# Chunk attention's values products on 128 keys by 128 queries, with block-diagonal probabilities, in a four-layer transformer kernel

## The chip, the cores and the metric

The kernel runs on one core of one Trainium2 chip. The metric is the device time of one launch in microseconds (us). The time before is 2157.64 us, the median of three runs (2156.42 to 2162.59).

## What is computed

The input is 16 sequences of 256 tokens with 128 features. Four attention blocks follow each other, each with a residual and a feed-forward block behind it: banded ("band"), causal, chunked ("chunk") and low-rank ("lowrank"). The chunk block has 16 heads of 8 features, and a token sees only the 64 tokens of its own chunk:

```python
B, T, C = x.shape            # 16, 256, 128
H, cs = (N_HEAD, CHUNK)      # 16, 64
d = C // H
nc = T // cs
...
scores = jnp.einsum('bnqhd,bnkhd->bnhqk', q, k) * scale
p = jax.nn.softmax(scores, axis=-1)
y = jnp.einsum('bnhqk,bnkhd->bnqhd', p, v)
y = y.reshape(B, T, C)
return jnp.einsum('btc,oc->bto', y, w_proj)
```

Two layers follow as `x + attention(layernorm(x))` and `x + ffn(layernorm(x))`; the second feed-forward block (behind chunk and lowrank) quantises its input and its hidden values to 4 bits in blocks of 16.

## The kernel before

A **unit** is one attention block of one sequence: 16 units each of band (B0 to B15 below), causal (C0 to C15), chunk (K0 to K15) and lowrank (L0 to L15), and 16 of "end" (E0 to E15), which hold only the last feed-forward. A unit first runs the feed-forward that precedes its attention ("forward" and "finish": `xT`, `ffn` 1 and 2, `hid`, for the quantised one `quant` and `ffn` 3, then `down`, `res`), then its queries, keys and values ("operands": `xn`, `xT`, `qk`, `rope`, `cast`, `stack`, `v`), the maxima of the scores ("maxima": `score` fills and DVE's reductions, then `parts`), the attention ("back": `nm`, the scores again as `S`, exponentials, the values products `V`), and the "tail" (`ctx`, `ctxT`, `out`). Units of different kinds run interleaved: while K5 is in its back, the forward of L3 runs.

**The order** of the steps on each engine is written out before the kernel is built. `make_plan` walks six queues (the stages) per engine with a table of assumed costs (`work`), the dependences (`needs`) and a table of leads (`LEAD`, one number for each engine, stage and kind of unit, and `PER_UNIT`), and picks each engine's next step. The engines then execute in that order; the assumed costs and the leads decide nothing else. Each PE step that fills PSUM takes one of three slots (`slots`, 1024 columns each), which the reader of the step frees. The values products write to `ctx_ps`, which the ACT step `V` copies to `ctxT`.

**Chunk attention's back**: for each of two 128-token tiles g, `scores` computes all 16 heads: for each head two 64x64 blocks (two chunks), keys on partitions, queries on columns, and on top the negated maxima (`nmT`, `pick`). One ACT instruction takes the exponentials of the whole 128x1024 slot to `probs[:, g % 2, 0]`. `values` then makes, for each head and each chunk, one product of 64 keys (rows) by 32 value columns by 64 queries: 32 products for a tile, 64 for a unit. The value columns hold 8 features and a column of ones, whose product is the denominator.

The trace shows a float32 product as two weight loads and two matmuls, and calls value buffers `band_va`, stacked queries and keys `band_r`. DVE's `nmx<-slots` is the maxima, `x<-slots` on L1317 the last step of an attention unit ("out"), POOL's L644 to L646 the last third of the 4-bit quantisation.

## Time and profile before

| | us |
|---|---|
| median of three runs (lowest to highest) | 2157.64 (2156.42 to 2162.59) |
| the profiled execution: its own time | 2152.07 |
| the profiled execution: span from first to last instruction | 2150.2 |
| PE matmul busy in the span | 1789.7 (83%) |
| PE weight loads busy | 1250.9 (58%) |
| DVE busy | 1345.8 (63%) |
| POOL busy | 978.6 (46%) |
| ACT busy | 808.8 (38%) |
| mean granted TensorE clock | 0.936 |

Shares of the whole span are averages over stages of different make-up; the rows further below are cut by stage. "issue" before a PE row is idle time in which PE waited for nothing that the profile shows. A row's "xcount" may merge instructions of one kind.

### The profile page before, as it was taken

What the parts mean: (1) busy time and instruction counts of PE and PEld (TensorE: products, weight loads), DVE (VectorE), ACT (ScalarE), POOL (GpSimd) and SP (SyncE); (2) the same over time, 40 slices, a digit from 0 to 9 for tenths busy, and PEclk for the clock granted to TensorE, in tenths of its full rate; (3) what the DMA queues carried; (4) which work ended last, traced back from release to release, by engine and by line L of the source; (5) the groups of instructions that cost most, each with busy time, mean ns of one, the idle gap of its engine ahead of it and who ended that gap; (6) DMA issues with size and microseconds to landing.
All of it is one profiled execution on the core that took longest, in us unless ns stands there. A gap on an engine that the chain in (4) does not pass through costs nothing.

```text
span 2150.2 us, 51747 instructions
## 1 busy us (share of the span) xinstructions
PE 1789.7 (83%) x21261; PEld 1250.9 (58%) x21261; DVE 1345.8 (63%) x2753; ACT 808.8 (38%) x1303; POOL 978.6 (46%) x1362
## 2 busy tenths in 40 slices
PE   4899889999999998879999997777776778888883
PEld 4566565666666666655555555667665455555553
DVE  4555555555555543574555555677876788888873
ACT  2333333333333332324444444333333444444441
POOL 3333222333332222453333435689997455555543
PEclk9999999999999999989999999888998788888886
DMA  4000000000000000023333332233443223323310
GB/s 161 1 1 1 1 2 1 1 1 1 1 1 1 1 1 1 16 56 74 64 78 71 75 75 61 60 74 78 91 87 65 46 62 65 65 65 65 65 21 8
DMA packets 167465, 89.54 MB, mean 42 GB/s; under 512 B 9393, under 2 KB 165810, under 8 KB 166978
## 3 DMA queue, kind: packets, MB, share of 16 engines
q1 hardware_dynamic: 167010, 85.70, 18.4%
q8 instruction: 172, 2.82, 0.6%
q14 instruction: 59, 0.48, 0.1%
q0 software_dynamic: 224, 0.54, 0.1%
HBM read 46.36 MB, written 39.85 MB: 40 GB/s over the span
## 4 chain that ended last, share of the span: by engine, by line
PE 51%; DVE 27%; ACT 7%; POOL 7%; issue 6%; DVEq 0%; POOLq 0%; ACTq 0%
PE slots L1327 38%; DVE nmx L1201 12%; PE ctx_ps L1327 10%; DVE rope_part L1242 4%; ACT probs L1087 3%; DVE rope_part L1166 2%; PE slots L1615 2%; ACT ctxT L1007 1%; DVE ctxT L1303 1%; DVE rope_part L1167 1%; POOL xn L922 1%; PE slots L1394 1%; ACT band_va L1023 1%; POOL band_rb L645 1%; DVE band_r L1167 1%
## 5 line engine op out<-in xcount | busy, mean ns | idle before, releaser
L1087 ACT ACTIVATE probs<-slots 128x1024 f32<-128x1024 f32 (+1 forms) x416 | 356.1, 892 | 322.0 <-PE slots L1327 318.8
L1201 DVE TENSOR_REDUCE nmx<-slots 128x8 f32<-128x1024 f32 (+2 forms) x352 | 407.7, 1216 | 102.8 <-PE slots L1327 101.2
L1327 PE MATMUL slots<-band_r 64*64 64x64 bf16 (+4 forms) x5120 | 393.6, 263 | 80.5 <-DVE nmx L1201 41.7
L1327 PEld LDWEIGHTS slots<-band_r 64*128 64x128 bf16 (+2 forms) x5120 | 194.6, 120 | 254.3 <-issue 129.8
L1242 DVE SCALAR_TENSOR_TENSOR rope_part<-slots,bias_qk,rope_band 128x256 f32<-128x256 f32 x512 | 212.3, 477 | 197.3 <-PE slots L1327 176.4
L1327 PE MATMUL ctx_ps<-probs,band_va 64*32 64x64 f32 (+4 forms) x5120 | 260.5, 313 | 42.3 <-issue 19.4
L986 POOL TENSOR_TENSOR band_r<-rope_part 128x512 f32<-128x512 f32 x128 | 164.5, 1285 | 250.9 <-DVE rope_part L1242 250.9
L1327 PE MATMUL slots<-mask,ident_bf 128*128 128x256 bf16 (+1 forms) x896 | 217.2, 324 | 46.9 <-DVE nmx L1201 17.7
L1327 PE MATMUL slots<-nmT,pick 64*128 64x256 bf16 (+2 forms) x2560 | 218.7, 241 | 2.7 <-issue 2.7
L1327 PEld LDWEIGHTS ctx_ps<-probs,band_va 128*32 128x32 f32 (+2 forms) x5120 | 145.3, 118 | 125.6 <-issue 62.8
L900 POOL TENSOR_TENSOR var_eps<-mean_var,eps 128x2 f32<-128x2 f32 x128 | 29.2, 228 | 393.4 <-DVE mean_var L1129 393.4
L1327 PE MATMUL slots<-xT,band_qk 128*128 128x256 f32 x1536 | 200.0, 288 | 8.2 <-DVEq L1248 6.1
L1327 PEld LDWEIGHTS slots<-xT,band_qk 128*128 128x128 f32 x1536 | 188.0, 191 | 19.7 <-DVEq L1248 13.6
L1007 ACT ACTIVATE ctxT<-ctx_ps 128x512 f32<-128x512 f32 (+1 forms) x112 | 87.4, 781 | 169.2 <-PE ctx_ps L1327 169.2
L922 POOL TENSOR_SCALAR band_va<-x,mean_var,rstd 128x128 f32<-128x128 f32 x128 | 100.8, 794 | 86.0 <-PE slots L1368 65.9
L1007 ACT ACTIVATE band_rb<-band_r 128x512 bf16<-128x512 f32 x128 | 79.4, 630 | 157.0 <-POOL band_r L986 157.0
L1327 PEld LDWEIGHTS slots<-mask,ident_bf 128*128 128x128 bf16 x896 | 54.9, 97 | 133.8 <-issue 44.9
L1166 DVE SCALAR_TENSOR_TENSOR rope_part<-band_va,slots 128x352 f32<-128x352 f32 (+2 forms) x128 | 68.6, 536 | 81.9 <-ACT band_va L1023 55.5
L1327 PEld LDWEIGHTS slots<-nmT,pick 64*128 64x128 bf16 (+1 forms) x2560 | 102.9, 104 | 11.5 <-issue 2.9
L922 POOL TENSOR_SCALAR xn<-x,mean_var,rstd 128x128 f32<-128x128 f32 x128 | 103.6, 816 | 2.9 <-POOL rstd L901 2.8
L937 POOL CAST nm<-nmx 128x64 bf16<-128x64 f32 x64 | 15.1, 236 | 179.0 <-PE slots L1573 92.7
L901 POOL TENSOR_TENSOR rstd<-var_eps,minus_half 128x2 f32<-128x2 f32 x128 | 91.5, 715 | 10.0
(181 smaller groups left out, 2947.5 us busy)
## 6 DMA issues: line engine op xcount, KB each, us to landing
band_r<-scratch SPq DMA_DIRECT2D x192, 192.0 KB, 4.5
scratch<-parts SPq DMA_DIRECT2D x96, 192.0 KB, 2.2
scratch<-parts SPq DMA_DIRECT2D x96, 128.0 KB, 2.1
scratch<-parts SPq DMA_DIRECT2D x96, 64.0 KB, 1.8
x<-in_x SPq DMA_DIRECT2D x16, 128.0 KB, 4.5
out<-x SPq DMA_DIRECT2D x16, 128.0 KB, 1.8
band_r<-in_band_qk_a SPq DMA_DIRECT2D x1, 1024.0 KB, 6.4
band_va<-in_band_qk_b SPq DMA_DIRECT2D x1, 1024.0 KB, 10.3
```

Source lines behind the costliest of these rows:

```text
L900: link(nc.gpsimd.tensor_tensor(var_eps[:, b], mean_var[:, b, :, 1], eps[:], ALU.add))
L901: nc.gpsimd.tensor_tensor(rstd[:, b], var_eps[:, b], minus_half[:], ALU.pow).then_inc(rstd_ready, 1)
L922: nc.gpsimd.tensor_scalar(xn[:, t, :], x[:, b, t, :], mean_var[:, b, t, 0:1], rstd[:, b, t:t + 1], ALU.subtract, ALU.mult).then_inc(xn_rea ...
L986: nc.gpsimd.tensor_tensor(band_r[:, b % RING, j], part[:, 0], part[:, 1], ALU.add).then_inc(band_sum, 1)
L1007: return nc.scalar.activation(dst, src, ACT.Copy)
L1087: nc.scalar.activation(probs[:, g % 2, step[2], :, 0:width], slot(u, step).rearrange("p (a n) -> p a n", a=2)[:, :, 0:width], ACT.Exp, sca ...
L1166: link(nc.vector.scalar_tensor_tensor(g_out, t_in, 1.0, gate, ALU.add, ALU.mult))
L1167: nc.vector.tensor_tensor(h_out, g_out, up, ALU.mult).then_inc(free_sem(u, ("ffn", i)), 1)
L1201: nc.vector.tensor_reduce(dst, src, axis=AX.X, op=ALU.max, negate=True).then_inc(free_sem(u, step), 1)
L1242: nc.vector.scalar_tensor_tensor(rope_part[:, c % 2, rot, qk, :], slot(u, step)[:, o:o + TOK], bias_qk[:, j, 2 * qk + rot:2 * qk + rot + 1 ...
L1327: return nc.tensor.matmul(o, lhsT, rhs, start=start, stop=stop, skip_group_check=shared)
L1615: last = nc.tensor.transpose(B[:, g * P:(g + 1) * P], ctxT[:, g, t * P:(t + 1) * P], ident[:])
```

## The change

A chunk unit's exponentials are now two ACT instructions of 64 partitions each, which lay the two chunks' probabilities of a head on the diagonal of a 128x128 block of `probs`; the other half of the block is zero, cleared once for both buffers by a POOL step ("blank") before the first chunk unit and never written again. A values product takes 128 keys by 128 queries for a head: 16 products for a tile where there were 32. ACT's copy of the result loses its permutation. The planner's assumed costs for chunk `S` on ACT and `V` on PE are changed, and every number of `LEAD` and `PER_UNIT`, so that the order of the steps changes from the first units on.

```diff
+FIRST_CHUNK = UNITS.index(("chunk", 0))
...
+        "blank": [("pool", 3.6)],
...
-              ("act", 0.49 if narrow else 0.92)],
-        "V": [("pe", {"band": 2.24, "causal": 0.79, "chunk": 0.61, "lowrank": 1.13}.get(kind))]
+              ("act", 0.49 if narrow else 1.9 if kind == "chunk" else 0.92)],
+        "V": [("pe", {"band": 2.24, "causal": 0.79, "chunk": 0.95, "lowrank": 1.13}.get(kind))]
...
+        if u == FIRST_CHUNK and step == ("S", 0, 0):
+            yield u, ("blank",), "pool"
...
+        if name == "blank":
+            yield FIRST_CHUNK - 1, LAST_V["causal"], "pe"
...
-        "finish": {"causal": -2.336, "chunk": -0.206, "lowrank": -0.262, "end": -0.693},
+        "finish": {"causal": -0.336, "chunk": -0.461, "lowrank": 0.349, "end": -0.388},
...
-PER_UNIT = 0.01
+PER_UNIT = 0.0024
...
+    at = stages["operands"].index((FIRST_CHUNK + 1, ("xn", False)))
+    stages["operands"][at:at] = [(FIRST_CHUNK, ("blank",))]
...
+        def probs_by_head(i):
+
+            return probs[:, i].rearrange("p f a n -> p (f a n)").rearrange("p (h c n) -> p h c n", h=HEADS, c=2)
+
...
+                    if step == ("blank",):
+                        pool.wait_ge(pv_done, gbase[FIRST_CHUNK])
+                        nc.gpsimd.memset(probs[:], 0.0).then_inc(probs_blank, 1)
...
+                        if kind == "chunk":
+                            if u == FIRST_CHUNK and step[1] == 0:
+                                act.wait_ge(probs_blank, 1)
+                            for c in range(2):
+                                rows = slice(c * CHUNK, (c + 1) * CHUNK)
+                                last = nc.scalar.activation(probs_by_head(g % 2)[rows, :, c].rearrange("p (h a) n -> p a h n", a=2),
+                                                            slot(u, step)[rows].rearrange("p (a h n) -> p a h n", a=2, n=CHUNK),
+                                                            ACT.Exp, scale=SD ** -0.5)
+                            last.then_inc(free_sem(u, step), 1)
+                            return
...
-                        elif kind == "chunk":
-                            copy(ctxT[:, 0:4, :].rearrange("p g (t c n) -> p c (g t) n", t=TILES, c=2),
-                                 ctx_ps[:].rearrange("p c (g n) -> p c g n", n=CHUNK)).then_inc(ctx_free, 1)
...
                         for h in range(HEADS):
-                            for cc in range(2):
-                                rows = slice(cc * CHUNK, (cc + 1) * CHUNK)
-                                o = ((h // 4) * TILES + g) * CHUNK
-                                last = mm(ctx_ps[32 * (h % 4):32 * (h % 4) + 32, cc, o:o + CHUNK],
-                                          small_va[rows, b % RING, g, h, :], pr[rows, 0, h % 2, h // 2 * CHUNK:(h // 2 + 1) * CHUNK])
+                            o = ctx_ps[32 * (h % 4):32 * (h % 4) + 32, h // 8, h // 4 % 2 * TOK + g * P:h // 4 % 2 * TOK + (g + 1) * P]
+                            last = mm(o, small_va[:, b % RING, g, h, :], probs_by_head(gi % 2)[:, h].rearrange("p c n -> p (c n)"))
                         last.then_inc(pv_done, 1)
```

What the new order does is seen in rows of the two programs, which give an instruction's line, its output and inputs, and how many follow each other. Line numbers of the changed kernel are higher, for the lines that were added.

**PE, a chunk unit in the middle of the stage, behind K7's `out`.** Before: the feed-forward products `ffn` 1 and 2 of L6 (`fp_gu`), `ffn` 3 of L5 (`ident,band_r`), the two `score` fills of K9 (64x64, x64), `down` of L5 (`fp_d`), then `nm` and the scores of K8:

```order
L1327 MATMUL slots<-fp_gu,xTf 128x352 x12
L1394 MATMUL slots<-ident,band_r 128x128 x2
L1394 MATMUL slots<-ident,band_r 96x128
L1394 MATMUL slots<-ident,band_r 128x128 x2
L1394 MATMUL slots<-ident,band_r 96x128
L1327 MATMUL slots<-band_r 64x64 x64
L1327 MATMUL slots<-fp_d,band_r 128x128 x6
L1573 MATMUL slots<-ident_bf,nm 128x128 x2
L1327 MATMUL slots<-band_r 64x64 x4
L1327 MATMUL slots<-nmT,pick 64x64 x4
```

In the changed kernel, at the same place (again behind K7's `out`):

```order
L1417 MATMUL slots<-ident,band_r 128x128 x2
L1417 MATMUL slots<-ident,band_r 96x128
L1417 MATMUL slots<-ident,band_r 128x128 x2
L1417 MATMUL slots<-ident,band_r 96x128
L1391 MATMUL slots<-ident,band_rb 128x128 x2
L1350 MATMUL slots<-fp_d,band_r 128x128 x6
L1350 MATMUL slots<-fp_gu,xTf 128x352 x12
L1593 MATMUL slots<-ident_bf,nm 128x128 x2
L1350 MATMUL slots<-band_r 64x64 x4
L1350 MATMUL slots<-nmT,pick 64x64 x4
```

`ffn` 3 and `down` of the older feed-forward now stand ahead of `ffn` 1 and 2 of the next one, and nothing stands between `ffn` 2 and `nm`; the two `score` fills are gone from here. The same unit, from the end of its scores to its `out`, before:

```order
L1327 MATMUL slots<-band_r 64x64 x4
L1327 MATMUL slots<-nmT,pick 64x64 x4
L1327 MATMUL slots<-band_r 64x64 x4
L1327 MATMUL slots<-nmT,pick 64x64 x4
L1327 MATMUL ctx_ps<-probs,band_va 32x64 x64
L1327 MATMUL slots<-chunk_qkv,xT 128x128 x6
L1368 MATMUL slots<-ident,xn 128x128 x2
L1615 MATMUL slots<-ident,ctxT 128x128 x8
L1327 MATMUL slots<-xT,chunk_qkv 128x256 x12
L1621 MATMUL slots<-ident,rope_part 128x128 x2
L1368 MATMUL slots<-ident,band_rb 128x128 x2
L1327 MATMUL slots<-chunk_o,ctxT 128x128 x2
```

And in the changed kernel:

```order
L1350 MATMUL slots<-band_r 64x64 x4
L1350 MATMUL slots<-nmT,pick 64x64 x4
L1350 MATMUL slots<-band_r 64x64 x32
L1350 MATMUL ctx_ps<-probs,band_va 32x128 x16
L1350 MATMUL slots<-band_r 64x64 x32
L1350 MATMUL ctx_ps<-probs,band_va 32x128 x16
L1350 MATMUL slots<-chunk_qkv,xT 128x128 x6
L1635 MATMUL slots<-ident,ctxT 128x128 x8
L1391 MATMUL slots<-ident,xn 128x128 x2
L1641 MATMUL slots<-ident,rope_part 128x128 x2
L1350 MATMUL slots<-xT,chunk_qkv 128x256 x12
L1350 MATMUL slots<-chunk_o,ctxT 128x128 x2
```

The 64 values products were in one run behind the scores; now each tile's 16 stand behind 32 products of a `score` fill of K9. `qk` of the operands (`xT,chunk_qkv`) moved behind `ctxT` (`ident,rope_part`), and the next `xT` of a feed-forward (`ident,band_rb`) out of this piece.

**PE, a causal unit, behind the first scores of C6.** Before, the `score` fills of C7 (a mask and 8 or 4 products each) have C6's first values step between the first and the second, and four `S` fills of C6 ahead of them:

```order
L1327 MATMUL slots<-mask,ident_bf 128x512 x2
L1327 MATMUL slots<-band_r 128x128 x8
L1327 MATMUL ctx_ps<-probs,band_va 32x256 x4
L1327 MATMUL ctx_ps<-probs,band_va 32x128 x4
L1327 MATMUL slots<-mask,ident_bf 128x512 x2
L1327 MATMUL slots<-band_r 128x128 x8
L1327 MATMUL slots<-mask,ident_bf 128x2x128 x2
L1327 MATMUL slots<-band_r 128x256 x4
L1327 MATMUL slots<-mask,ident_bf 128x2x128 x2
L1327 MATMUL slots<-band_r 128x256 x4
L1327 MATMUL slots<-mask,ident_bf 128x2x128 x2
L1327 MATMUL slots<-band_r 128x256 x4
```

In the changed kernel all six stand in one run, behind the second `S` fill of C6 and ahead of the third:

```order
L1350 MATMUL slots<-mask,ident_bf 128x512 x2
L1350 MATMUL slots<-band_r 128x128 x8
L1350 MATMUL slots<-mask,ident_bf 128x512 x2
L1350 MATMUL slots<-band_r 128x128 x8
L1350 MATMUL slots<-mask,ident_bf 128x2x128 x2
L1350 MATMUL slots<-band_r 128x256 x4
L1350 MATMUL slots<-mask,ident_bf 128x2x128 x2
L1350 MATMUL slots<-band_r 128x256 x4
L1350 MATMUL slots<-mask,ident_bf 128x2x128 x2
L1350 MATMUL slots<-band_r 128x256 x4
L1350 MATMUL slots<-mask,ident_bf 128x2x128 x2
L1350 MATMUL slots<-band_r 128x256 x4
```

What moved is that run. Beside it, by C0's `out` PE has issued all 16 feed-forwards that precede causal units before, and in the changed kernel 8 and the first half of a ninth; from there on each causal unit has one whole feed-forward, where before every second one had.

**POOL, where causal goes over to chunk.** Before, the normalisation and casts for the next units follow each other:

```order
L957 TENSOR_TENSOR rope_part<-rope_part,small_d 128x512
L900 TENSOR_TENSOR var_eps<-mean_var,eps 128x2
L901 TENSOR_TENSOR rstd<-var_eps,minus_half 128x2
L922 TENSOR_SCALAR band_va<-x,mean_var,rstd 128x128 x2
L900 TENSOR_TENSOR var_eps<-mean_var,eps 128x2
L901 TENSOR_TENSOR rstd<-var_eps,minus_half 128x2
L991 TENSOR_TENSOR small_d<-rope_part,parts 128x512
L995 TENSOR_TENSOR parts<-small_d,parts 128x512
L922 TENSOR_SCALAR xn<-x,mean_var,rstd 128x128 x2
```

In the changed kernel the clearing of `probs` stands among them:

```order
L914 TENSOR_TENSOR rstd<-var_eps,minus_half 128x2
L913 TENSOR_TENSOR var_eps<-mean_var,eps 128x2
L914 TENSOR_TENSOR rstd<-var_eps,minus_half 128x2
L977 MEMSET probs 128x4096
L935 TENSOR_SCALAR xn<-x,mean_var,rstd 128x128 x2
L935 TENSOR_SCALAR band_va<-x,mean_var,rstd 128x128 x2
L913 TENSOR_TENSOR var_eps<-mean_var,eps 128x2
L914 TENSOR_TENSOR rstd<-var_eps,minus_half 128x2
L950 CAST nm<-nmx 128x4x16
```

POOL waits there for C15's last values product; `xn` of K1 and, four steps on, the maxima's `parts` of K0 (`nm<-nmx`) are queued behind it.

## Rows read from the trace of the kernel before

**Rows 1.** Windows: busy us of each engine (x instructions), granted clock, DMA, by stretch.
```profile
core 0: us, PE busy (x) PEld busy (x) DVE busy (x) ACT busy (x) POOL busy (x), PEclk, DMA share, GB/s
852.55:981.06 128.51, 104.96 (x970) 80.91 (x968) 79.12 (x191) 38.45 (x79) 56.60 (x84) 0.95 0.18 38
981.06:1268.59 287.53, 262.27 (x3090) 156.08 (x3088) 164.85 (x299) 133.03 (x216) 110.01 (x172) 1.00 0.35 73
...
1375.42:1479.56 104.14, 77.79 (x1936) 69.63 (x1934) 77.56 (x182) 38.13 (x69) 88.27 (x118) 0.84 0.35 75
1479.56:1573.94 94.38, 70.61 (x1940) 61.54 (x1940) 77.34 (x181) 38.36 (x70) 89.73 (x121) 0.95 0.43 87
1573.94:1662.12 88.18, 63.14 (x1492) 55.41 (x1492) 61.67 (x148) 32.27 (x59) 71.78 (x96) 0.86 0.37 77
...
1757.88:2029.09 271.21, 220.53 (x2222) 143.49 (x2221) 228.06 (x382) 134.27 (x200) 153.66 (x220) 0.87 0.31 64
```

**Rows 2.** The chain within K6's `out` to K11's, shares by line.
```profile
by line: issue 14.4%; POOL band_rb L645 11.0%; POOL band_rb L644 9.9%; POOL xn L922 8.9%; POOL band_r L646 8.4%; POOL rstd L901 6.6%; POOL rope_part L957 6.6%; POOL parts L995 6.1%; POOL band_va L922 4.4%; POOL nm L939 4.3%; POOL band_va L6
```

**Rows 3.** Timeline of a chunk unit's exponentials and values products (K5).
```profile
1447.91 1.98 ACT L1087 ACTIVATE probs<-slots 128x1024 f32<-128x1024 f32 x2 [0.89 <-PE slots L1327]
...
1449.08 1.31 PE L1327 MATMUL ctx_ps<-probs,band_va 64*32 64x64 f32 x93 [0.33 <-ACT probs L1087]
...
1452.94 0.85 PE L1327 MATMUL ctx_ps<-probs,band_va 64*32 64x64 f32 x35 [2.55 <-issue]
...
1453.82 1.02 ACT L1007 ACTIVATE ctxT<-ctx_ps 128x1024 f32<-128x1024 f32 x1 [3.94 <-PE ctx_ps L1327]
```

**Rows 4.** Chain pieces "issue" (start, us): first, longest and last of ten.
```profile
1384.38 1.38 issue
...
1605.24 2.57 issue
...
1629.93 1.61 issue
```

**Rows 5.** Timeline of PE between K7's `ffn` 2 and K8's `nm`.
```profile
1519.92 0.82 PE L1394 MATMUL slots<-ident,band_r 128*128 128x128 f32 x6
1520.79 0.45 PE L1327 MATMUL slots<-band_r 64*64 64x64 bf16 x32
1521.97 0.45 PE L1327 MATMUL slots<-band_r 64*64 64x64 bf16 x32 [0.73 <-DVE band_r L1167]
1522.43 1.58 PE L1327 MATMUL slots<-fp_d,band_r 128*128 128x128 f32 x12
1523.84 0.28 PE L1573 MATMUL slots<-ident_bf,nm 128*128 128x128 bf16 x2
```

**Rows 6.** Timeline: values products of chunk, lowrank and causal.
```profile
1507.80 0.77 PE L1327 MATMUL ctx_ps<-probs,band_va 64*32 64x64 f32 x55 [0.74 <-ACT probs L1087]
...
1937.99 1.07 PE L1327 MATMUL ctx_ps<-probs,band_va 128*32 128x256 f32 x16 [0.20 <-ACT probs L1087]
...
1051.55 0.86 PE L1327 MATMUL ctx_ps<-probs,band_va 128*32 128x256 f32 x16
```

**Rows 7.** Groups by shape: ACT's, POOL's clearing, DVE's maxima, the feed-forward's products.
```profile
L1087 ACT ACTIVATE probs<-slots 128x1024 f32<-128x1024 f32 x288 | 285.5, 1024 | 254.4 <-PE slots L1327 253.6
L1087 ACT ACTIVATE probs<-slots 128x512 f32<-128x512 f32 x128 | 76.1, 594 | 67.7 <-PE slots L1327 65.2
L1007 ACT ACTIVATE xTf<-slots 128x256 fp32r<-128x256 f32 x64 | 24.6, 384 | 65.4 <-PE slots L1368 65.3
L1007 ACT ACTIVATE band_r<-slots 96x256 f32<-96x256 f32 x32 | 12.1, 380 | 1.0
L966 POOL MEMSET band_r<- 128x4096 f32 x1 | 3.5, 3503 | 0.0
L1201 DVE TENSOR_REDUCE nmx<-slots 128x4 f32<-128x1024 f32 x256 | 296.7, 1215 | 22.3 <-PE slots L1327 20.9 <-DVE rope_part L1258 0.2 <-DVE band_va L643 0.2
L1327 PE MATMUL slots<-xTf,int_gu 128*128 128x256 f32 x384 | 59.9, 305 | 2.9 <-DVE nmx L1201 1.8 <-DVE xTf L1142 0.2
L1327 PE MATMUL slots<-int_d,rope_part 128*128 128x128 f32 x384 | 53.8, 294 | 4.5 <-DVE rope_part L1167 3.8 <-DVE x L1317 0.3 <-DVE ctxT L1303 0.2
```

**Rows 8.** PE's waits, 852.55 to 981.06.
```profile
PE slots L1327 <- DVE rope_part L1167: 14.4, 12, 1.5
```

**Rows 9.** PE's waits, 981.06 to 1268.59.
```profile
PE slots L1327 <- DVE nmx L1201: 9.6, 30, 0.4
```

More of the change, by code:

```diff
@@ L293 @@
     "pe": {
[L294 to L299 removed]
+        "tail": {"band": 0.237, "causal": 0.056, "chunk": 19.523, "lowrank": 0.573},
@@ L314 @@
     },
     "pool": {
[L316 to L320 removed]
+        "tail": {"band": -26.537, "causal": 14.799, "chunk": -11.625, "lowrank": -2.754},
@@ L321 @@
+        "finish": {"causal": 14.734, "chunk": -11.243, "lowrank": -38.395, "end": 18.275},
+        "forward": {"causal": 8.144, "chunk": 43.134, "lowrank": 20.054, "end": 10.219},
+        "operands": {"band": -38.777, "causal": 11.083, "chunk": 20.032, "lowrank": 9.358},
+        "maxima": {"band": -0.85, "causal": 2.543, "chunk": -51.021, "lowrank": 24.839},
     },
 }
-PER_UNIT = 0.01
+PER_UNIT = 0.0024
 def released_by(u, step):
```

35 lines of the change are left out of this document (15 added, 20 removed).

## The prediction, made before the changed kernel ran

> **What bounds the kernel now.** I read the page's shares first, then cut the span at the last steps of the attention units (the 64 residual additions on L1317) and read busy time, clock, waits and chain for each stretch. The page's 83% for PE says little: by stretch [rows 1] PE is 91% busy in causal attention (981.06 to 1268.59) at full clock, 82% in the stretch before it, in which most feed-forwards ahead of causal attention run, and only 72% to 75% in the chunk stage. There the reader should look at POOL. From K6's last step to K11's (1479.56 to 1573.94) five units take 94.38 us, 18.9 us each, POOL is 95% busy, and the chain goes through POOL's quantisation and normalisation [rows 1, 2]. The five units before and the four behind take 104.14 and 88.18 us, 21.4 us each, with POOL at 85% and 81%: something else paces these. In the lowrank stage (1757.88 to 2029.09) DVE is busy 84% and PE 81%, neither all the time.
>
> What paces the nine slower units is seen in K5 [rows 3]. PE runs the values products of both tiles, stops with 35 records left and sits 2.55 us in which it waits for no semaphore. The chain of 1375 to 1662 has ten such pieces above 1 us outside the POOL stretch, from 1.08 to 2.57 us, 18.6 us together [rows 4]. That nearly fills the gap to POOL's pace: 9 x (21.4 - 18.9) = 22 us. They come within or just before the values products, that is behind some 500 records of very small products in a row; I read them as PE running out of instructions, which the trace suggests and does not prove.
>
> **The change, part by part.** The sum is made against the profiled execution's own 2152.07 us; the median of the runs is 5.6 us higher, and the difference is carried over.
>
> (a) *The exponentials.* Each tile's one instruction of 1024 elements per partition becomes two with half the partitions. The trace has no 64-partition exponential. Time goes by elements per partition: 1024 take 1024 ns, 512 take 594 ns, and a copy of 256 takes 384 ns on 128 partitions and 380 on 96 [rows 7]. So the cost of a half is between 0.51 us (if half the partitions halved it) and 1.02 us; I take 1.0. A unit's exponentials last 4.0 us instead of 1.98, ACT gains 32 us in all, and at 37% to 41% busy in these stretches [rows 1] it has room; what counts is the delay of PE's last values product.
>
> (b) *The values products.* A tile of the old form takes 0.77 us for the 55 records that one row shows, some 0.86 us for 64 [rows 6]. The new form is 16 products of 128 columns, 2048 columns, on 128 rows. Lowrank's values step has 8 products of 256 columns, the same 2048, on the same rows, and takes 1.07 us; causal's with 1536 columns takes 0.86 [rows 6]. I take 1.07 us: +0.2 us a tile, +7 us of PE in 32 tiles, hidden where POOL paces. The lower bound is 0.86 (half as many records, no loss), the upper 1.72, if PE had run two 64-row products at a time and now can't.
>
> (c) *What the two do to the path.* In K5 from the start of the exponentials to the start of ACT's copy it is 5.91 us [rows 3]. In the changed kernel it is 4.0 + 1.07, 5.1 us, if PE does not run dry: the wait for instructions is replaced by a wait for ACT. With the mean stall of 18.6/9 = 2.1 us instead of 2.55 the old path is 5.4 us, and the gain 0.3 to 0.4 us. I expect the stall to go: the unit has 128 records fewer, and the ones left come with pauses for the exponentials between them. `score` products fill one such pause each.
>
> (d) *The new order in the chunk stage.* Between `ffn` 2 and `nm` PE spends 3.9 us on `ffn` 3, `score`, a 0.73 us wait for DVE, `score` and `down` [rows 5]. Now `nm` follows `ffn` 2 directly. `ffn` 3 and `down` (0.8 and 1.4 us) stand ahead of `ffn` 1, the `score` fills in ACT's shadow: about 1.7 us shorter. The scores of the unit may then wait for a slot that DVE still reads, so I count 1.2 us. (c) and (d) give 1.6 us x 9 units = **-14 us**. The ceiling is POOL's pace, -22, since POOL's own work of 89.73/5 = 17.9 us a unit is untouched; the floor is nothing. At POOL's pace the five middle units gain nothing.
>
> (e) *Clearing `probs`.* POOL's clearing of 4096 columns is there once at 3.5 us [rows 7]. It now waits for C15's last values product, and K1's normalisation and K0's maxima parts are queued behind it; PE waits for the latter at `nm`. PE has three feed-forward pieces to do meanwhile. Bounds 0 and 7 us (the clearing and as much again queued behind); **+2 us**.
>
> (f) *Feed-forwards moved out of the stretch before causal attention.* PE waits there 14.4 us for DVE's gated product (`rope_part` L1167) [rows 8], for 16 feed-forwards, 0.9 each. Seven and a half of them move to causal units, each with other work of PE about it: **-7 us**. Their own PE work (59.9 and 53.8 us for 32, 3.6 us each [rows 7]) moves along and costs the same. Bounds 0 and -14.
>
> (g) *Six maxima in a row in the causal units.* DVE needs 6 x 1.215 = 7.3 us for them [rows 7] and there are three slots, so PE's third scores fill waits until DVE has done the fourth. Before, PE idled (287.53 - 262.27)/13 = 1.9 us a unit [rows 1], of which 9.6/13 = 0.7 for the maxima [rows 9]. I add 0.3 us a unit, **+4 us**; bounds nothing and the idle time doubled, +25.
>
> (h) *Lowrank.* `ffn` 3 and `down` leave the tail of a unit and stand at its head, with one or two more maxima there. What is saved behind the values products is added before `nm`: **0**, bounds one maximum a unit over 13 units, 16 us either way. In the band stage the same steps have the same neighbours but for a few: 0.
>
> Sum: -14 + 2 - 7 + 4 = **-15 us**: 2137 for the profiled execution, **2143 us** against the median.
>
> **The rivals.** *The exponentials surface (slower).* The place is the wait of the last values product for ACT. For it speaks that PE already waits there 0.7 us in K8 [rows 6], although ACT is half as busy as it will be. If 2.0 us of ACT and 2 x 0.2 us of PE add to each of 14 units while the stalls go, it is 34 - 18.6 = +15, with (e), (f), (g) +14: 2172. Against it: DVE has quantisation and maxima to do before it needs the result. It decides once 6 units' worth (14/2.4) is exposed.
>
> *The pace is held elsewhere (no change).* DVE is at 74% in the first five chunk units and POOL at 85% [rows 1]; they may form a loop with PE that keeps 21 us without any stall. Then (c) and (d) give nothing, and (e) to (g) cancel: 2151 to 2161, I say 2157.
>
> *Runs of maxima (slower).* (g) at its upper bound and (h) at +16, with the rest as forecast: +22 beside a gain of 19, or 36 us above the forecast: 2179. DVE is the busier engine in lowrank, which speaks for it; in causal it is 57% busy, which speaks against.
>
> *The row halves.* If the old products ran two at a time, (b) is at its upper bound, 0.65 us a tile more than I count; exposed in the nine slower units and a few others, 11 x 1.3 = 14 us: 2157, no change. The old record pace of 0.77 us for 55, 14 ns a record, speaks for some overlap; that the lowrank form is about as fast by column speaks against. The Trainium skill ("TensorEngine Tiling (Array Packing)", Theoretical Speedup) says that a small dimension of at most 64 can give up to 2x when the array is split, which the change gives up; no row here shows the new form.
>
> **How the numbers follow.** Forecast 50%, exponentials 14%, held pace 20%, maxima 10%, row halves 6%. Within 0.3% (6.5 us), about what runs of this kernel can tell from no change, lie the second rival of no change and the row halves, less a little: faster 0.51, same 0.25, slower 0.24. The forecast's own range is its terms between their likelier bounds, 2125 to 2151. The range for all reaches up to the exponentials' 2172 and a little beyond, and leaves out the maxima's case and a gain above 38 us: 2120 to 2175.
>
> **What the changed profile would show.** (a) ACT rows of 64x1024 near 1.0 us. (b) `ctx_ps` rows 128*32 128x128, 1.07 us a tile. (c) no "issue" pieces above 1 us in the chunk stage, and its units at 19 to 20 us with POOL near 95% throughout. (e) `nm` of K0 not waiting for POOL. (f) the stretch to C0's last step shorter by some 35 us, with causal units of about 23.5 us, each with a feed-forward. (g) PE's waits for `nmx` in causal at 1 us a unit. The prediction fails if the stalls stay with half the values records, if POOL isn't the bound once they are gone, or if the lowrank units, a quarter of the time, move by half a microsecond each.

## The result, and the profile of the changed kernel

The changed kernel takes 2200.48 us (median of 4 runs, 2194.85 to 2204.09), the kernel before 2158.09 beside it: ratio 1.0195, interval 1.0176 to 1.0214. It is slower by 42 us, where 15 us less were forecast, and lies outside the range. Two executions further below, one of 5190.25 and one of 3254.23 us, fell in a much slower state of the chip and are in no median and no ratio.

Columns as in [rows 1]; first the changed kernel's page, then its windows between the same steps: the stretch before causal, causal (C0 to C13), the crossing (C13 to K4), K4 to K11, K11 to K15, K15 to L2, L2 to L12.

```profile
span 2196.9 us, 49731 instructions
...
PE 1819.0 (83%) x20237; PEld 1264.5 (58%) x20237; DVE 1350.5 (61%) x2753; ACT 839.9 (38%) x1335; POOL 976.0 (44%) x1363
```
```profile
864.03:966.24 102.21, 84.35 (x776) 62.50 (x774) 59.53 (x128) 30.74 (x60) 45.84 (x64) 0.93 0.21 47
966.24:1286.04 319.80, 285.37 (x3261) 175.42 (x3260) 186.83 (x365) 142.52 (x235) 123.71 (x196) 1.00 0.31 66
1286.04:1481.21 195.17, 146.62 (x2273) 118.53 (x2271) 116.48 (x274) 75.45 (x128) 109.85 (x159) 0.86 0.28 58
1481.21:1628.64 147.43, 108.53 (x2266) 91.66 (x2267) 110.22 (x252) 67.38 (x111) 119.34 (x169) 0.90 0.36 77
1628.64:1720.29 91.65, 66.88 (x1242) 55.56 (x1240) 64.66 (x150) 40.60 (x69) 69.13 (x94) 0.85 0.33 71
1720.29:1804.52 84.23, 64.23 (x657) 40.13 (x657) 66.61 (x126) 38.06 (x57) 47.78 (x71) 0.86 0.26 58
1804.52:2076.01 271.49, 218.96 (x2221) 146.34 (x2222) 229.64 (x380) 132.22 (x200) 154.82 (x220) 0.89 0.30 64
```

The stretch before causal is 26 us shorter and causal 32 us longer than in [rows 1]: feed-forwards moved from one to the other (776 records of PE for 970, 3261 for 3090). The surprise lies at the chunk stage and its entry. At K4's last step, where PE has done the same work in both orders, the changed kernel is at 1481.2 us and the one before at 1440.2: all but 6 us of the span's 47 are lost by then. And no five chunk units come near POOL's pace.

The new instructions are as costed, by shape [rows 7 have those of before] (of the first row's 1536 records 1024 are the new products, the others were there before), and PE's waits show more for the maxima in the causal stretch [rows 9]; the last two lines are from the stretch before causal [rows 8]:

```profile
L1350 PE MATMUL ctx_ps<-probs,band_va 128*32 128x128 f32 x1536 | 69.0, 299 | 14.2 <-ACT probs L1108 13.9
L1108 ACT ACTIVATE probs<-slots 64x1024 f32<-64x1024 f32 x64 | 65.2, 1018 | 14.5 <-PE slots L1350 13.8
L977 POOL MEMSET probs<- 128x4096 f32 x1 | 3.5, 3517 | 6.8 <-PE ctx_ps L1350 6.8
```
```profile
PE slots L1350 <- DVE nmx L1224: 18.0, 52, 0.4
PE slots L1350 <- DVE rope_part L1190: 8.5, 13, 0.7
```
```profile
PE slots L1391 <- DVE rope_part L1190: 5.5, 4, 1.7
PE slots L1350 <- DVE rope_part L1190: 2.6, 3, 1.4
```

What [rows 3] showed in K5 is still there, only in another place. PE in K10 of the changed kernel (start, us, what; idle time before it in brackets):

```profile
1591.50 0.22 PE L1350 MATMUL slots<-nmT,pick 64*64 64x64 bf16 x4
1594.52 0.27 PE L1350 MATMUL slots<-band_r 64*64 64x64 bf16 x4 [2.80 <-issue]
...
1595.52 1.93 PE L1350 MATMUL ctx_ps<-probs,band_va 128*32 128x128 f32 x32
1597.38 0.49 PE L1350 MATMUL slots<-band_r 64*64 64x64 bf16 x30
1598.96 0.22 PE L1350 MATMUL slots<-band_r 64*64 64x64 bf16 x2 [1.09 <-issue]
1599.11 1.08 PE L1350 MATMUL ctx_ps<-probs,band_va 128*32 128x128 f32 x32
```

The stall of 2.80 us now falls among `S`, ahead of the values products, and a second one inside `score` 1. The clock can be seen too: 32 records of values take 1.93 us behind the long stall, at a granted clock of 0.50, and the same 32 take 1.08 us when they come again 3.6 us later, at 1.00.

### The profile page after: what moved, and what is told of

Read it like the earlier page. It is cut to its first block, busy times and chain, and to the rows that moved or that the text cites. A ratio compares the mean times of both kernels' runs of the same rounds, so it can differ in the third digit from the quotient of the medians.

```text
span 2196.9 us, 49731 instructions
## 1 busy us (share of the span) xinstructions
PE 1819.0 (83%) x20237; PEld 1264.5 (58%) x20237; DVE 1350.5 (61%) x2753; ACT 839.9 (38%) x1335; POOL 976.0 (44%) x1363
## 4 chain that ended last, share of the span: by engine, by line
PE 51%; DVE 33%; ACT 6%; issue 5%; POOL 4%; DVEq 0%; POOLq 0%; ACTq 0%
PE slots L1350 38%; DVE nmx L1224 12%; PE ctx_ps L1350 8%; DVE rope_part L1265 6%; DVE rope_part L1189 3%; PE slots L1635 2%; DVE rope_part L1190 1%; ACT probs L1113 1%; DVE ctxT L1326 1%; DVE band_r L1190 1%; ACT band_va L1039 1%; ACT ctxT L1023 1%; DVE band_rb L648 1%; PE slots L1391 1%; DVE band_rb L645 1%
## 5 line engine op out<-in xcount | busy, mean ns | idle before, releaser
L1350 PE MATMUL slots<-band_r 64*64 64x64 bf16 (+4 forms) x5120 | 402.5, 269 | 78.2 <-DVE nmx L1224 30.4
L1113 ACT ACTIVATE probs<-slots 128x1024 f32<-128x1024 f32 (+1 forms) x384 | 322.2, 881 | 271.5 <-PE slots L1350 268.7
L1350 PEld LDWEIGHTS slots<-band_r 64*128 64x128 bf16 (+2 forms) x5120 | 201.6, 124 | 252.1 <-issue 142.2
L1350 PE MATMUL ctx_ps<-probs,band_va 128*32 128x256 f32 (+3 forms) x4096 | 269.2, 346 | 18.9 <-ACT probs L1108 13.9
L1350 PEld LDWEIGHTS ctx_ps<-probs,band_va 128*32 128x32 f32 (+1 forms) x4096 | 151.1, 121 | 99.4 <-issue 48.2
L1207 DVE SCALAR_TENSOR_TENSOR x<-slots,x 128x256 f32<-128x256 f32 x64 | 27.0, 422 | 166.4 <-PE slots L1350 165.8
L653 POOL TENSOR_TENSOR band_rb<-band_rb 128x352 f32<-128x352 f32 x64 | 59.7, 932 | 86.3 <-DVEq L1200 83.5
```

The lines of the kernel that those rows point to most:

```text
L653: lambda at, blocks: v.tensor_tensor(qx[:, at], qx[:, at], qp[:, at], ALU.add),
L1113: nc.scalar.activation(probs[:, g % 2, step[2], :, 0:width], slot(u, step).rearrange("p (a n) -> p a n", a=2)[:, :, 0:width], ACT.Exp, sca ...
L1350: return nc.tensor.matmul(o, lhsT, rhs, start=start, stop=stop, skip_group_check=shared)
```

## The experiments

Four questions: products or order; where in the order; what in the causal and chunk units; and whether a better order exists. Ratios are to the kernel before on the same chip. Differences in us are differences of ratios, times the 2157 us of the kernel before; an interval of ±0.002 is ±4 us.

### Products or order

**The new order with the old products.** ScalarE's and TensorE's chunk code of before in the changed kernel, the order untouched:

```diff
-                            last = mm(o, small_va[:, b % RING, g, h, :], probs_by_head(gi % 2)[:, h].rearrange("p c n -> p (c n)"))
+                            for cc in range(2):
+                                rows = slice(cc * CHUNK, (cc + 1) * CHUNK)
+                                o = ((h // 4) * TILES + g) * CHUNK
+                                last = mm(ctx_ps[32 * (h % 4):32 * (h % 4) + 32, cc, o:o + CHUNK],
+                                          small_va[rows, b % RING, g, h, :], pr[rows, 0, h % 2, h // 2 * CHUNK:(h // 2 + 1) * CHUNK])
```

> The changed kernel's order of steps on every engine (its leads and assumed costs, and the clearing of probs), but the chunk exponentials, values products and the copy as before. If the order costs the 42 us, this is within 10 us of the changed kernel: 2190 to 2205 us. If the new products and exponentials cost it, this is at 2158 us or below, since the order alone shortens the stretch before C0's last step. If both share it, about 2180. Causal units should be 24.5 us each by every theory, since nothing of them differs from the changed kernel.

Measured: 2214.53 us, ratio 1.0274 (1.0238 to 1.0310). The order alone costs 59 us, more than any of the forecasts.

**The old order with the new products.** LEAD, PER_UNIT and the assumed costs of before; the clearing is put by hand on POOL behind K0's parts:

```diff
+ORDER["pool"].insert(ORDER["pool"].index(("front", FIRST_CHUNK + 2, ("rope",))), ("front", FIRST_CHUNK, ("blank",)))
```

> The order of before on every engine, to the step, with the new exponentials, products and copy; the clearing of probs stands on POOL behind K0's maxima parts. If the order is the cause, this is at 2158 us or a little below or above (the ACT halves cost up to 2 us a unit, the stalls behind the values products shrink): 2145 to 2165. If the products are the cause, 2190 to 2200: each of 16 units 2 to 2.5 us longer.

Measured: 2149.99 us, ratio 0.9968 (0.9951 to 0.9985). In this order the products gain 7 us; so with them the order loses 49. In the new order they gain 17 (1.0274 to 1.0195).

**The exponentials' split alone**, in the kernel before, each tile's exponential as two instructions on 64 partitions:

```diff
+                        if kind == "chunk":
+                            for c in range(2):
+                                rows = slice(c * CHUNK, (c + 1) * CHUNK)
```

> The kernel before with one edit: a chunk tile's exponentials are two instructions of 64 partitions, to the same places as before. If the longer exponentials are hidden behind PE's stalls and POOL's pace: within 5 us of 2158. If they surface in every unit: 16 x 2 = 32 us more, 2190.

Measured: 2170.56 us, ratio 1.0073 (1.0041 to 1.0105), +16 us, between the two forecasts.

**The products alone**, in the kernel before: 16 products of 128 by 128 a tile on probabilities that are not block-diagonal (the sums mix the two chunks), with one exponential:

```diff
-                            for cc in range(2):
...
+                            o = ctx_ps[32 * (h % 4):32 * (h % 4) + 32, h // 8, h // 4 % 2 * TOK + g * P:h // 4 % 2 * TOK + (g + 1) * P]
+                            last = mm(o, small_va[:, b % RING, g, h, :], pr[:, 0, h % 2, h // 2 % 4 * P:(h // 2 % 4 + 1) * P])
```

> The kernel before with one edit: 16 values products of 128 keys by 128 queries a tile, on the probabilities as they lie (so the sums mix chunks: the output of chunk attention is not the reference's), with one exponential instruction a tile. It has half of the values records and no longer exponential. If fewer records shrink PE's stalls: the nine slower chunk units come down toward 18.9 us, 2140 to 2150. If the stalls only move to other records: 2158, or up to 7 us more for the longer products.

Measured: 2141.92 us, ratio 0.9928 (0.9901 to 0.9955), -15.5 us. Split and products would add up to about 0, where -7 was measured for both; the sum is known to ±10 us, so 0 and -7 are not told apart. PE's waits between K1's last step and K15's show where the time goes; of each line the total, the number and the longest. The kernel before, then the old order with the new products:

```profile
PE ctx_ps L1327 <- issue: 19.1, 14, 2.6
PE ctx_ps L1327 <- ACT probs L1087: 7.7, 13, 0.7
PE slots L1327 <- issue: 7.4, 6, 2.5
```
```profile
PE ctx_ps L1345 <- ACT probs L1103: 28.4, 24, 1.8
...
PE slots L1345 <- issue: 5.3, 3, 2.3
```

The waits for nothing fall from 26.5 us in 20 pieces to 5.3 in 3, and the wait for the exponentials takes their place, 7.7 to 28.4 us. In that order seven of the eleven units K2 to K12 reach 18.6 to 19.0 us, POOL's pace. In the run with the exponentials split the same view has 30.8 us for `probs` and 10.0 us of issue (13 pieces), with the products alone 7.2 us of issue (8). So the split alone, with every values record kept, takes away most of the waits for nothing too, and puts more waiting for ScalarE in their place than it saves. In the new order the waits for nothing are 34.0 us (21 pieces) with the old products and 13.6 us (7) with the new.

### Where in the order

The next kernels hold both plans and join them at a unit's last step on TensorE (new products everywhere). At B12 and K4 TensorE has then done the same steps in both orders; at C13 two steps differ and at K11 one:

```diff
+PARTS = [("old", ("causal", 13)), ("new", ("chunk", 4)), ("old", None)]
...
+    for which, last in PARTS:
+        plan, plan_slots = plans[which]
+        for entry in plan:
+            eng, half, u, step = entry
+            if entry not in taken:
+                taken.add(entry)
+                log.append(entry)
...
+            if last and (eng, u, step) == ("pe", UNITS.index(last), ("out",)):
+                break
```

**New up to K4, old behind** (`[("new", ("chunk", 4)), ("old", None)]`):

> The changed kernel's order up to unit K4's last step, then the order of before; products, exponentials and copy as changed everywhere. At that step TensorE stands at the same instruction number in both orders, so no work is moved across the seam. Theory A (the loss lies where the traces lost it: 41 us before K4's last step, 8 us behind it against the order of before with the new products): 1481 us up to K4 and the 707 us that the order of before took from there, a span of 2188, a ratio to the kernel before of 1.017 to 1.020. Rival (the loss is a debt that the order before K4 leaves behind, and paid back in the lowrank units by the rest of the new order): over 1.023, since the pay back is taken away. Rival (the loss is in the steady chunk units alone, from K4 on, the rest being work done earlier or later): under 1.005.

Measured: 2180.89 us (three executions), ratio 1.0130 (1.0098 to 1.0163). The interval lies below what theory A gave and far above the rival of the steady units: 35 us over the old order, 14 less than the changed kernel. The only profile of this run is of the execution of 5190.25 us and is not read.

**Old up to K4, new behind** (`[("old", ("chunk", 4)), ("new", None)]`):

> The mirror: the order of before up to unit K4's last step, then the changed kernel's. Theory A: 1440 us up to K4 and the 716 us that the changed kernel took from there, a span of 2155, ratio 1.001 to 1.004, with chunk units of 20.1 to 21.7 us behind K4 and an issue piece on TensorE in most of them. Rival (steady chunk units carry the loss): 1.010 or more. Rival (the loss behind K4 is only an echo of what lies ahead): 0.997, as with the order of before throughout.

Measured: 2154.71 us, ratio 0.9995 (0.9972 to 1.0017): 6 us over the old order, a little under theory A's ratio; the interval reaches down to the rival's 0.997. K5 to K13 take 19.2 to 21.6 us, but for two of 26.

**New in the stretch before causal and in causal** (`[("old", ("band", 12)), ("new", ("causal", 13)), ("old", None)]`):

> The changed kernel's order only from band unit B12's last step to causal unit C13's last step; the order of before on both sides, products as changed. Theory A (the six maxima in a row cost more than the emptied stretch before the causal units gives back: 26 us less, 32 us more): a span of 2153 to 2156, ratio 1.000 to 1.003, if the seam at C13 costs nothing. Rival (causal units of 24.5 us are only the moved feed-forwards, none of it loss): 2147, ratio 0.997. Rival (the new order leaves a worse start for the chunk units): over 1.006.

Measured: 2159.99 us, ratio 1.0019 (1.0003 to 1.0034): 11 us over the old order, as theory A gave, or a little more.

**New in the crossing** (`[("old", ("causal", 13)), ("new", ("chunk", 4)), ("old", None)]`):

> The changed kernel's order only from C13's last step to K4's last step, that of before on both sides, products as changed. In the changed kernel this stretch took 195.2 us, with the order of before and the new products 167.3. Theory A (the crossing from causal to chunk units is itself the largest part of the loss): 28 us more than the 2150 of the order of before, 2172 to 2180, ratio 1.007 to 1.011. Rival (the crossing was long because the causal units ahead of it had left other work for it): at most 10 us more, ratio under 1.002.

Measured: 2174.92 us, ratio 1.0086 (1.0068 to 1.0104): 25 us over the old order, half of the loss. Its window, and behind it the one between the same steps in the old order with the new products:

```profile
1272.70:1464.65 191.95, 141.68 (x2246) 114.06 (x2246) 113.59 (x268) 74.75 (x126) 108.76 (x157) 0.88 0.30 59
```
```profile
1272.22:1439.55 167.33, 130.99 (x2246) 105.61 (x2244) 111.51 (x268) 74.10 (x126) 109.07 (x157) 0.93 0.33 68
```

The work is the same to the record, 2246 of PE and 268 of DVE. PE idles 50.3 us for 36.3, and its same records are busy 10.7 us longer, at a granted clock of 0.88 for 0.93. So this order is paid for twice: in waits, and in more time at the slower of TensorE's two levels (1.2 for 2.4 GHz). The two parts are not equally firm. In twelve traces with the old order and the new products between these steps the stretch takes 162 to 173 us, PE idle 36.3 to 38.8 of them and busy 124.4 to 136.1. So 12 to 14 us are waits whichever is compared, and 6 to 17 us longer busy time.

**New in the bands** (`[("new", ("band", 12)), ("old", None)]`):

> The changed kernel's order only up to band unit B12's last step, then the order of before; products as changed. Theory A (the parts of the loss add up: 8 us in the bands, 10 in the causal stretch, 25 in the crossing, 5 behind K4): 2158, ratio 0.999 to 1.002. Rival (the bands' loss seen in one trace is drift or is made up at the seam): 2150, ratio 0.997.

Measured: 2158.04 us, ratio 1.0008 (0.9994 to 1.0023): 8.6 us over the old order. The four parts give 8.6 + 11 + 25.4 + 5.8 = 51 us for the 49 lost, though the first three together, in the run that is new up to K4, gave 35 and not 45. By the intervals the first comparison is known to ±14 us and the second to ±12, so neither says whether the parts add up. That the bands lose is firmer: B12's last step comes at 760 to 769 us in sixteen traces with the old order there, and at 777 to 779 in three with the new one. Between B4's last step and B12's PE has the same 3522 records; it idles 28.4 us for 25.8 (it now waits 6.2 us for ScalarE's `band_rb`) and is busy 383.1 for 378.9.

**The one place where the new order is faster:** from K11 on (568 us to the end for 573), `[("old", ("chunk", 11)), ("new", None)]`:

> The order of before up to unit K11's last step, then the changed kernel's: the one stretch where the new order was not slower (from K11 to the end 568 us against 573). Theory A: a span of 2142 to 2143, ratio 0.993 to 0.996. Rival (the gain behind K11 is only what the units ahead had already done): 0.997 or more.

Measured: 2140.43 us, ratio 0.9930 (0.9907 to 0.9952), 8 us under the old order with the new products and faster than both kernels.

### The maxima in a row

In this group and the next, steps are moved by hand, and the program then also deals the three slots out anew, by the planner's own rule. 25 to 170 of the 1747 fills so get their slot from another step than in the run that they are compared with. Most of these stand at the moved steps, but in the three runs that leave TensorE's order as it was (maxima ahead of `xq`, POOL's `res`, VectorE's line) it is 54, 32 and 25. No run changed the slots alone, so each result is of the move and the slots together.

**Fills interleaved with scores and values**, in the kernel with the new order in causal:

```diff
+        score = [("front", u + 1, ("score", i)) for i in range(6)]
+        back = [("back", u, step) for step in (("S", 1, 0), ("S", 1, 1), ("V", 0), ("S", 2, 0), ("S", 2, 1), ("V", 1))]
+        at = pe.index(score[0])
+        if pe[at:at + 12] == score + back:
+            pe[at:at + 12] = [x for pair in zip(score, back) for x in pair]
```

> As the run with the new order in the band to causal stretch alone (2160 us), but on TensorE the six score fills of the next causal unit stand one by one between six steps of this unit's scores and values (score 0, S 1.0, score 1, S 1.1, score 2, V 0, score 3, S 2.0, score 4, S 2.1, score 5, V 1), the same work in other places. Theory G (the fills in a row wait for VectorE's maxima, 5.8 us of each unit's chain, and this is what a causal unit of 24.5 us is long for): causal units of 23.3 us or less, 14 us or more off the total, about 2145. Rival (TensorE is 89% busy there and hands the wait on: the maxima end when VectorE has done them, six times 1.2 us behind one another, wherever the fills stand): units of 24.5 us, 2158 to 2162. Rival (values products wait for exponentials that now come later): units over 24.8.

Measured: 2149.47 us, ratio 0.9967 (0.9954 to 0.9980), 11 us less than without the edit. PE's wait for the maxima in this stretch, without and with it:

```profile
PE slots L1413 <- DVE nmx L1287: 16.6, 48, 0.4
```
```profile
PE slots L1461 <- DVE nmx L1335: 8.0, 12, 0.7
```

Waits for exponentials come in, 5.2 us in 13 pieces. Six causal units take 143.8 us for 146.9, 0.5 us each, less than the 1.2 expected; from C0's last step to C13's it is 7 us (317.7 for 324.7 us). The other 4 us are not in the moved steps' stretch: behind C13, where both have the order of before, the two traces differ by 10 us (875 for 885), and only the slots of a few fills differ.

**The same in the old order**, for the four fills that stand in a row there, on top of the version that was fastest:

```diff
+            mixed = [score[0], back[0], score[1], back[1], score[2], back[2], score[3]]
```

> The fastest version so far (order of before up to K11, then the changed kernel's: 2140.4 us) with the score fills 2 to 5 of a causal unit interleaved with S 2.0, S 2.1 and V 1 on TensorE, in the order of before too. Theory G (fills in a row wait for maxima): the new order's causal units gained 0.5 us each by it; with four fills instead of six in a row 0.2 to 0.5 us in each of 13, 2134 to 2138, ratio 0.989 to 0.991. Rival (four in a row are hidden): 2140.

Measured: 2132.13 us, ratio 0.9889 (0.9872 to 0.9906), the fastest kernel of all, and more than expected. Its causal window (C1 to C13), and PE's waits for maxima in it:

```profile
1002.10:1255.90 253.80, 239.00 (x2846) 143.75 (x2844) 154.12 (x277) 123.24 (x199) 100.83 (x159) 1.00 0.38 76
```
```profile
PE slots L1463 <- DVE nmx L1337: 1.5, 5, 0.3
```

The wait of 9.6 us [rows 9] is down to 1.5, and six units take 126.5 us for 131.9.

**All six alternating**, `range(6)` and the six steps of the new order's edit:

> As the fastest version (order of before up to K11 with score fills 2 to 5 of a causal unit interleaved: 2132.1 us), but all six score fills of a causal unit alternate with S 1.0, S 1.1, V 0, S 2.0, S 2.1 and V 1. Theory G (what counts is that no two fills stand in a row): another 1 to 4 us, 2128 to 2131. Rival (scores 0 and 1 ahead now delay the exponentials of group 1, and values wait for them): 2133 to 2140.

Measured: 2133.59 us, ratio 0.9888 (0.9868 to 0.9908): no difference to four in the total, though C1 to C13 takes 251.6 us for 253.8.

### What makes a chunk unit of the new order 21 us long

Base: old up to K4, new behind (2154.71 us; K5 to K13 take 21.7 us each on average). **Score fills ahead of `nm`**, as in the old order:

```diff
+        at = pe.index(("back", u - 1, ("nm",)))
+        pe[at:at] = score
```

> As the run with the new order behind K4 alone (2154.7 us; its chunk units take 20.1 to 21.7 us, those of the order of before 18.7), but on TensorE both score fills of the next chunk unit stand ahead of nm again, for K5 to K14. VectorE's order stays: their maxima behind hid 1 and 2, xq and quant 0 and 1. Theory L (a chunk unit of the new order is a loop of VectorE's line low, hid, xq, quant, score, ctx and TensorE's way from ctx back to low): VectorE still comes to the maxima at the same time, so no gain: 2153 to 2160. Rival I (the units are long since TensorE runs out of instructions among the small products, and the score fills between them make it worse): units of 19.5 us or less, 2140 or less.

Measured: 2158.89 us (nine executions), ratio 1.0019 (0.9998 to 1.0039), units of 21.3 to 22.3 us, again 21.7 on average. Between K5's last step and K11's no wait for nothing is left, where the base had 10.9 us; PE waits 15.4 us for exponentials there instead, for 3.1. **And the maxima ahead of `xq` and `quant`** on VectorE:

```diff
+        at = dve.index(("front", u + BATCH - 2, ("xq", 0)))
+        dve[at:at] = score
```

> As the run before, and on VectorE the two maxima stand ahead of xq and quant 0 and 1 again. Theory L: the loop is cut by the 2.4 us of the maxima, and POOL's pace of 18.7 us is in reach: chunk units of 18.7 to 19.6 us in nine units, 15 to 20 us off 2154.7, so 2135 to 2140, ratio 0.990 to 0.993. Rival I (instruction supply): the nm, scores and values of a unit stay behind one another as they were, so the gaps and the 21 us units stay: 2150 or more.

Measured: 2164.76 us, ratio 1.0040 (1.0019 to 1.0060), units of 20.6 to 24.3 us. My loop through VectorE's maxima was not what held the unit. The chain now comes through the feed-forward: POOL's last quantisation, then `ffn` 3, which stands ahead of `ffn` 1 in the new order (start, us, what):

```profile
1589.19 0.79 POOL band_r L770
1590.11 0.86 PE slots L1532 x6
1590.99 0.61 ACT band_r L1138
1592.15 2.55 PE slots L1465 x18
```

The rival, that TensorE runs out of instructions, is no better: the issue waits did go or shrink, the units did not get shorter. Between K5's last step and K11's, base first, then this run:

```profile
PE slots L1413 <- issue: 10.9, 5, 2.5
```
```profile
PE slots L1465 <- issue: 2.8, 2, 2.6
```

**`ffn` 3, `down` and `res` moved back too:**

```diff
+        third = [("front", ahead - 2, ("ffn", 3)), ("front", ahead - 2, ("down",))]
...
+        pe[at:at] = third[:1] + score + third[1:]
...
+        act.insert(act.index(("front", ahead - 1, ("ffn", 2))) + 1, third[0])
```

> As the run with scores and maxima ahead (2164.8 us, chunk units of 21.9 us on average, their chain running through the feed-forward's quant 2 on POOL and then its third step ffn 3 on TensorE), but for K5 to K14 ffn 3 and down of the unit before also stand behind ffn 1 and 2 of this unit again, on TensorE and ScalarE, and res on VectorE behind xq: the work of quant 2 then lies beside ffn 1 and 2. Theory F (ffn 3 ahead of the next ffn 1 chains two feed-forwards behind one another, and a chunk unit is as long as that chain): units of 18.7 to 19.6 us, 15 to 25 us off, 2140 to 2150, ratio 0.992 to 0.997. Rival (instructions run out among the small products whatever the order): units of 21 us and more, 2160.

Measured: 2183.52 us, ratio 1.0106 (1.0068 to 1.0144), units of 22.0 to 25.3 us. TensorE has no issue wait between K5 and K10, and the units are longer than ever. POOL, whose order still is the new one, waits for the statistics of `res`, with `quant` 2 queued behind:

```profile
POOL var_eps L1034 <- DVE mean_var L1273: 28.0, 5, 6.3
```

**POOL's `res` behind `quant` 2 as well:**

```diff
+        pool.remove(res)
+        pool.insert(pool.index(("front", ahead - 2, ("quant", 2))) + 1, res)
```

> As the run with the third step behind (2183.5 us, chunk units of 22 to 25 us, in which POOL waited 5.7 us a unit for the statistics of the feed-forward's res, with quant 2 queued behind that wait), but on POOL res stands behind quant 2, for K5 to K14. Theory F (a chunk unit of the new order is as long as the loop through the feed-forward's steps, and that loop is only cut when TensorE, VectorE and POOL all work one feed-forward apart): units of 18.7 to 19.8 us, 2140 to 2152, ratio 0.992 to 0.998. Rival (another loop of about 21 us lies behind it, as behind the two edits before): units of 20.5 to 22 us, 2155 to 2168.

Measured: 2175.89 us, ratio 1.0091 (1.0062 to 1.0120), units of 21.1 to 24.7 us behind a first one of 19.6. That wait of POOL's is gone. What stays is VectorE's wait for the gate of the feed-forward (`hid`), which ScalarE passes on late. It came in with the edit before, 19.2 us there against 1.2 in the run with the maxima ahead, and is now:

```profile
DVE rope_part L1313 <- ACT band_va L1165: 16.3, 5, 3.8
```

Four edits, and none brought the units below the base's 21.7 us (21.7, 21.9, 23.8 and 22.6 on average); each time other waits filled the gap. Neither the stalls nor the loop through `ffn` 3 is shown to be the cause; which pair of steps holds the new order's unit stays open.

**VectorE's line in the crossing**, on the kernel with the new order from C13 to K4: maxima of K4 and `low` 0, `rope` of K6 ahead of `quant` 0 and 1:

```diff
+    at = dve.index(("front", FIRST_CHUNK + BATCH + 1, ("quant", 0)))
+    dve[at:at] = moved
```

> As the run with the new order from C13 to K4 alone (2174.9 us, of which unit K4 takes 39.6), but on VectorE the maxima of K4, and low 0 and rope of K6, stand ahead of quant 0 and 1 of the feed-forward L1 and not behind or between. In the trace TensorE waits 4.4 us in one piece for low 0 there. Theory V (VectorE's line and TensorE's line take turns in this unit): 4 to 9 us off, 2166 to 2171. Rival (the unit is long because it holds two whole feed-forwards, whose quant steps only move behind the maxima): 2173 to 2177.

Measured: 2171.40 us, ratio 1.0067 (1.0044 to 1.0091) for 1.0086; the intervals overlap. The unit K4 itself went from 39.6 to 46.2 us and others got shorter, so this supports nothing. What makes the crossing long is open beyond the split above into waits and longer busy time.

## Why the prediction was wrong

- **(a) the exponentials**: right. 1018 ns each for 1.0 us, so half the partitions save nothing against the 1024 ns of [rows 7].
- **(b) the values products**: right. 1.08 us a tile at full clock for 1.07.
- **(c) what the two do to the path**: the mechanism was right and the size small. In the old order the stalls go, ScalarE's wait replaces them, and 7 us come off, where 0.3 to 0.4 us in nine units were 3. The rival of the exponentials was half right too: the split alone costs 16 us. Both reasons given for the stall's going hold in the old order, since the fewer records alone and the pauses alone each take most of it away (26.5 us to 7.2 and 10.0). In the new order PE still waits 13.6 us for nothing in seven pieces over the chunk stage.
- **(d) the new order in the chunk stage**: this is the step that failed. It costed only what stands between `ffn` 2 and `nm` on PE, 1.2 us a unit saved, as if VectorE and POOL had their results ready at the earlier time. Units of 19 to 20 us were expected; K4 to K11 takes 147.4 us, 21.1 each, where the old order with these products took 134.6, 19.2 each. Nor was the stall what held them: without any wait for nothing between K5 and K11 the new order's units there took 21.6 us still, and POOL, busy 81% from K4 to K11, was not the bound. Worse, but for the clearing the sum had no term at all for the crossing from C13 to K4: +25 us. Why the engines' orders cost this much there stays open.
- **(e) clearing `probs`**: in keeping. 3.5 us, and `nm` of K0 has no wait for POOL.
- **(f), (g) feed-forwards and six maxima**: -3 us together were expected, +11 us measured. Before causal 26 us came off for the 35 expected, and causal units take 24.5 us for 23.5. (f) failed as a mechanism: the wait for the gated product moved along with the feed-forwards. It was 14.4 us before; now it is 8.1 (5.5 + 2.6) in the stretch before causal and 8.5 in causal, so nothing was saved where 7 us were counted. The wait for maxima is 18.0 us, 1.4 a unit for the 1 expected; interleaving them gave back 7 us in the causal units and 11 by the ratios. So (g) was mis-sized, at 4 us for 7 to 11, within its bounds.
- **(h) lowrank**: right, 271.5 for 271.2 us. "In the band stage the same steps have the same neighbours but for a few: 0" was wrong by 8.6 us: four band units take 204.5 or 205.7 us for 202.2, again part wait and part longer busy time.
- **The held pace** rival came nearest: it said that engines form a loop that keeps 21 us without any stall, which is what the units of the new order did. That DVE and POOL form it is not shown. It was priced as no gain, with nothing for the crossing.

The idle time of PE rose by 17 us over the span and its busy time by 29, with 1024 records fewer. A sum made of waits alone, as mine was, misses the second.

The Trainium skill ("TensorEngine Tiling (Array Packing)", Theoretical Speedup) gives up to 2x for a dimension of at most 64 in a split array. Here a tile of 32 split products took 0.86 us at full clock and one of 16 whole ones 1.08, so the split was worth 1.26x by time in the array, and the version without it was still the faster kernel (ratio 0.9928), with 32 records fewer a tile and most of the stalls gone.

## What to carry to other kernels

When a change comes with a new order, run the order and the change apart before costing either: here they were -7 and +49 us. Cost an order by what each engine waits for in the units where the kind of work changes, not only in steady units, and join two orders at a step where one engine has done the same work in both, or nearly: that divided the loss in five runs and found a kernel faster than both (0.9930). Fills that one engine makes and another reduces should alternate with other work once they outnumber the buffers: here four or six fills stood in a row for three slots, and alternating them gave 11 and 9 us (0.9889).

## What the hardware showed

- TensorE stopped for 1 to 2.8 us, waiting for nothing that the profile shows, behind some hundred small products in a row. In the chunk stage of the old order these waits were 26.5 us, with half the values records 7.2, with the exponentials split and every record kept 10.0, with both 5.3; in the new order 34.0 and 13.6. With the score fills ahead of `nm` they went from 10.9 us to none in six units, and no time was gained.
- The queue that the profile calls instruction moved 172 packets before and 164 after, each of 16384 bytes. TensorE has 1024 matmuls and 1024 weight loads fewer and the other engines about as many instructions as before, so it looks like TensorE's own: 64 bytes an instruction, by this estimate. In seven traces (the kernel before, the changed kernel, the four runs on products or order, the base of the chunk units) all 57 such stops above 1 us ended 1.0 to 1.7 us behind the end of one of these packets; such moments make up about a tenth of the time. That TensorE waits for its instructions fits all of this; no run changed the fetching itself.
- Stretches with more waits also ran at a lower clock: 2246 equal records cost 131.0 us at a granted clock of 0.93 and 141.7 us at 0.88, and 32 equal records of values 1.08 us at 1.00 and 1.93 us at 0.50.
- An exponential of 1024 columns takes 1018 ns on 64 partitions, 1024 on 128.
